# A layernorm, sparse-FFN, layernorm kernel: threshold steps moved to ScalarE and GpSimd within one stage, a shorter pipeline, and a reordered fill

## The reference, cut to what matters

```python
# x: (8, 512, 512) = 4096 tokens of 512
x = layernorm(x + x @ (W + delta_W).T)                       # LN1
z = x @ ternary_quant(W_syn).T + b_syn                       # 2048 wide
topv, _ = top_k(z, 204); thresh = topv[:, -1:]
hidden = where(z >= thresh, relu(z), 0.0)
out = hidden @ ternary_quant(W_out).T + b_out
x = layernorm(layernorm(x + out) * gamma + beta + x)         # LN2, residual, LN3 (no affine)
# ternary_quant(W): -1, 0 or +1 times mean(|W|), split at half that mean
```

## Time and profile before

| | us |
|---|---|
| median of 3 runs | 695.01 (693.21 to 698.05) |
| the profiled execution | 695.96 |
| span of its trace, first to last instruction | 694.2 |
| busy in the span: PE, DVE, ACT, POOL | 589.0, 537.7, 525.3, 349.2 |

### The profile page before, as it was taken

One profiled execution on the slowest core, in us unless ns is written; L12 is line 12 of the kernel. 1 busy time (PEld: TensorE's weight loads), 2 busy tenths in 40 slices (PEclk: granted clock), 3 DMA queues, 4 the chain that ended last, 5 costly groups with the idle time before them and its releaser, 6 DMA issues.

```text
span 694.2 us, 8155 instructions
## 1 busy us (share of the span) xinstructions
PE 589.0 (85%) x2374; PEld 256.9 (37%) x2374; DVE 537.7 (77%) x646; ACT 525.3 (76%) x659; POOL 349.2 (50%) x721
## 2 busy tenths in 40 slices
PE   0578896999999999999999999999999988055573
PEld 0233342444444444444444444444444433022221
DVE  4671856688888888888888888888888898677751
ACT  3436477679989988998888998998998988864322
POOL 0202731246556556556556556556556566565631
PEclk9877897999999999999999999999999999577786
DMA  9931121446464546464445554546444453233351
GB/s 343 389 100 47 22 55 36 85 77 112 101 122 91 123 69 143 70 134 87 110 89 121 91 122 91 123 91 122 92 91 93 91 92 76 45 77 76 78 104 46
DMA packets 184480, 71.61 MB, mean 103 GB/s; under 512 B 168048, under 2 KB 176240, under 8 KB 183792
## 3 DMA queue, kind: packets, MB, share of 16 engines
q1 hardware_dynamic: 184432, 71.07, 46.5%
HBM read 20.72 MB, written 8.39 MB: 42 GB/s over the span
## 4 chain that ended last, share of the span: by engine, by line
PE 28%; POOL 19%; issue 18%; DVE 6%; DMA 3%; ACT 1%; DVEq 0%; POOLq 0%; ACTq 0%
PE z_ps L805 8%; PE o_ps L821 8%; PE o_ps L815 8%; POOL nmean L328 4%; PE u_ps L791 4%; POOL rs L337 3%; DMA hT<-hh 3%; POOL x1b L345 2%; POOL b L340 2%; DVE m L650 2%; POOL x1g L349 1%; DVE w_sb L645 1%; DVE z_sb L703 1%; DVE hh L639 1%; ACT hh L504 1%
## 5 line engine op out<-in xcount | busy, mean ns | idle before, releaser
L480 ACT ACTIVATE junk<-z_sb,t_col 128x2048 f16<-128x2048 f32 x128 | 254.8, 1992 | 41.1 <-POOL t_col L383 41.1
L805 PE MATMUL z_ps<-t_syn,xhT 128*128 128x512 f16 x1024 | 226.2, 379 | 0.6 <-issue 0.6
L791 PE MATMUL u_ps<-weff,xT_sb 128*128 128x512 f32 x256 | 132.8, 667 | 32.8 <-DVE weff L578 16.8
L805 PEld LDWEIGHTS z_ps<-t_syn,xhT 128*128 128x128 f16 x1024 | 100.0, 98 | 131.8 <-issue 18.5
L345 POOL TENSOR_TENSOR x1b<-x1s,vecs 128x512 f32<-128x512 f32 x32 | 42.8, 1339 | 198.7 <-DVE z_sb L703 198.6
L815 PE MATMUL o_ps<-t_out,hT 128*128 128x512 f16 x512 | 123.6, 397 | 6.7 <-DMA hT<-hh 6.7
L821 PE MATMUL o_ps<-t_out,hT 128*128 128x512 f16 x512 | 117.4, 383 | 3.4 <-DMA hT<-hh 3.4
L669 DVE SCALAR_TENSOR_TENSOR z_sb<-z_ps,sc,bias_z 128x1024 f32<-128x1024 f32 x64 | 81.6, 1278 | 49.6 <-PE z_ps L805 49.6
L703 DVE SCALAR_TENSOR_TENSOR z_sb<-z_sb,thr 128x2048 f32<-128x2048 f32 x32 | 75.3, 2352 | 31.8 <-issue 16.3
L639 DVE TENSOR_TENSOR hh<-z_sb,hh 128x2048 f16<-128x2048 f32 x32 | 84.5, 2639 | 3.2 <-ACT hh L504 3.2
L791 PEld LDWEIGHTS u_ps<-weff,xT_sb 128*128 128x128 f32 x256 | 51.5, 212 | 89.6 <-issue 88.6
(11 more groups left out here) (114 smaller groups left out, 514.4 us busy)
## 6 DMA issues: line engine op xcount, KB each, us to landing
xT_sb<-in_xT SPq DMA_DIRECT2D x16, 512.0 KB, 4.8
out_y<-y_sb SPq DMA_DIRECT2D x32, 256.0 KB, 2.3
z_sb<-in_w_synT SPq DMA_DIRECT2D x4, 1024.0 KB, 13.0
z_sb<-in_w_outT SPq DMA_DIRECT2D x2, 1024.0 KB, 18.7
hh<-in_w_outT SPq DMA_DIRECT2D x2, 1024.0 KB, 13.7
weff<-in_wT SPq DMA_DIRECT2D x1, 1024.0 KB, 5.5
w_sb<-in_dwT SPq DMA_DIRECT2D x1, 1024.0 KB, 7.7
bias_z<-in_b_syn SPq DMA_DIRECT2D x1, 1024.0 KB, 17.4
```

Of the source, the lines that this page charges most:

```text
L480: a_.activation(junk[:, done[0] % 2, :], z_sb[:, t % ZS, :], ACT.Sign, bias=bias, scale=-1.0, accum_out=signs[:, t % CS:t % CS + 1]).then_ ...
L791: last = mm(u_ps[:, :], xT_sb[:, j, k, (t % 2) * P:(t % 2 + 1) * P], weff[:, k, :], start=k == 0, stop=k == KD - 1)
L805: last = mm(z_ps[:, c, b * BANK:(b + 1) * BANK], xhT[:, j, h * KD + k, :], t_syn[:, k, n0:n0 + BANK], start=k == 0 and h == 0, stop=k == K ...
```

## The change

- Lags. The threshold of a tile is found within one stage (only the fifth count falls in the next), so `L_SEL, L_MM3, L_LN2, L_OUT` go from 4, 5, 6, 7 to 2, 3, 4, 4 and the last stage from 38 to 35. `A_LN1` is 3.
- Threshold. The first two moves are made by ACT itself, one ACTIVATE on 128x1 each (`first_step`, `second_step`), with no damping and no gate. POOL makes the third and fourth (`update(t, 2)`, `update(t, 3)`) for the one tile, in 5 and 7 instructions, the gate in the last one only. `T_MIN` is gone and `SPREAD` is 1.295.
- Means. `mean_r` and `mean_v` take the place of `means`; POOL no longer waits for `hidden`.
- DVE order in a stage: `below`, `top8`, `lo_x`, `select`, `centre`, `general`, `hidden`, `add_v`, `evac` of the first half, `lo_h`, `evac` of the second, `add_r`.
- PE order: first half of `mm2`, `mm3_hi`, `flags`, `mm3_lo`, second half of `mm2`, `mm1`. The flag goes to the second half of `z_ps`.
- SP order: `transpose_x` of s+1, then both transposes of tile s-2, then the store.
- Fill, written out by hand. ACT makes Sign of W_syn plus the lower bound (`sign_syn`, 128x1024, fp16), DVE the part under it times -1, and an fp16 `tensor_tensor` max joins both. One of four |W_out| sums and the scaling of `vecs` move to DVE. The ternary of W_out is placed among the first tiles' work.

```diff
...
@@ -31,22 +31,21 @@
...
 ROUNDS = 5
-SPREAD = 1.2965
+SPREAD = 1.295
...
-L_SEL, L_MM3, L_LN2, L_OUT = 4, 5, 6, 7
-A_LN1, A_MM1 = 2, 3
-FIRST, LAST = -A_MM1, TILES - 1 + L_OUT
-ZS, XS, OS, CS = 6, 9, 3, ROUNDS
+L_SEL, L_MM3, L_LN2, L_OUT = 2, 3, 4, 4
+A_X, A_LN1, A_MM1 = 1, 3, 3
+LAST = TILES - 1 + L_OUT
+ZS, XS, OS = 6, 8, 3
...
-            for s in range(FIRST, LAST + 1):
-                if live(s - L_MM3):
-                    transpose_lo(s - L_MM3)
-                if s % 2 and 2 <= (s + 5) // 2 < PAIRS:
+            transpose_x(0)
+            load(2)
+            for s in range(LAST + 2):
+                if s % 2 and (s + 5) // 2 < PAIRS:
                     load((s + 5) // 2)
-                if live(s + A_LN1):
-                    transpose_x(s + A_LN1)
-                if live(s - L_OUT):
-                    store(s - L_OUT)
+                if live(s + A_X):
+                    transpose_x(s + A_X)
                 if live(s - L_SEL):
                     transpose_hi(s - L_SEL)
+                    transpose_lo(s - L_SEL)
+                if live(s - 1 - L_OUT):
+                    store(s - 1 - L_OUT)
             for j in range(2):
...
-            def means(s):
-                j, d, e = s % 2, s - L_LN2, s - L_OUT
-                wait(pool, r_made, upto(d))
-                wait(pool, v_made, upto(e))
-                wait(pool, sq_done[1], upto(d - 2))
-                wait(pool, sq_done[2], upto(e - 2))
-                g.tensor_scalar(nmean[:, j, :], sums[:, j, :], -1.0 / D, None, ALU.mult).then_inc(neg_means, 1)
+                g.tensor_scalar(start[:, 3:4], start[:, 2:3], SIGN_MID, start[:, 1:2], ALU.mult, ALU.add).then_inc(sigma_step, 1)
...
+            def mean_r(t):
+                pool.wait_ge(r_made, t + 1)
+                wait(pool, sq_done[1], t - 1)
+                g.tensor_scalar(nmean[:, 0, t % 2:t % 2 + 1], sums[:, 0, t % 2:t % 2 + 1], -1.0 / D, None, ALU.mult)\
...
+            def mean_v(t):
+                pool.wait_ge(v_made, t + 1)
+                wait(pool, sq_done[2], t - 1)
+                g.tensor_scalar(nmean[:, 1, t % 2:t % 2 + 1], sums[:, 1, t % 2:t % 2 + 1], -1.0 / D, None, ALU.mult)\
...
-                    g.tensor_tensor(b3[:, j:j + 1], nmean[:, j, 1:2], rs[:, j, 2:3], ALU.mult).then_inc(b3_ready, 1)
+                    pool.wait_ge(v_mean, e + 1)
+                    g.tensor_tensor(b3[:, j:j + 1], nmean[:, 1, e % 2:e % 2 + 1], rs[:, j, 2:3], ALU.mult).then_inc(b3_ready, 1)
...
+            def second_base(t):
...
+                pool.wait_ge(t_first, t + 1)
+                g.tensor_tensor(base[:, t % 2:t % 2 + 1], t_col[:, t % 2, 1:2], start[:, 4:5], ALU.add).then_inc(base_made, 1)
+            def update(t, r):
...
+                j = t % 2
+                signed, new, old = signs[:, j, r:r + 1], dev[:, j, r:r + 1], dev[:, j, r - 1:r]
+                before = slope[:, j, r - 1:r] if r > 2 else start[:, 2:3]
...
+                if r == 2:
+                    pool.wait_ge(counted, count_no(t, 1))
+                    made_old = step(g.tensor_scalar(old, signs[:, j, r - 1:r], SIGN_MID, None, ALU.add))
+                    pool.wait_ge(update_step, made_old)
+                pool.wait_ge(counted, count_no(t, r))
+                crossed = step(g.tensor_scalar(q[0], signed, SIGN_MID, old, ALU.add, ALU.mult))
+                made_dev = step(g.tensor_scalar(new, signed, SIGN_MID, None, ALU.add))
...
+                damp = step(g.tensor_scalar(q[1], q[0], 0.0, -DAMP, ALU.is_lt, ALU.mult))
+                move = new
+                if r == ROUNDS - 2:
+                    pool.wait_ge(update_step, made_dev)
+                    squared = step(g.tensor_scalar(q[2], new, new, None, ALU.mult))
...
+                damped = step(g.tensor_scalar(slope[:, j, r:r + 1], q[1], before, before, ALU.mult, ALU.add))
+                if r == ROUNDS - 2:
+                    pool.wait_ge(update_step, squared)
+                    move = q[3]
+                    far = step(g.tensor_scalar(move, q[2], GATE ** 2, new, ALU.is_gt, ALU.mult))
+                    pool.wait_ge(update_step, far)
+                    wait(pool, selected, t - 1)
+                else:
+                    pool.wait_ge(t_second, t + 1)
+                    pool.wait_ge(update_step, damped)
+                g.tensor_scalar(t_col[:, j, r + 1:r + 2], move, slope[:, j, r:r + 1], t_col[:, j, r:r + 1],
+                                ALU.mult, ALU.add).then_inc(updated[r - 2], 1)
+                pool.wait_ge(updated[r - 2], t + 1)
...
+            scales(-3)
+            bias_norm()
+            scales(-2)
+            sigma()
+            scales(-1)
+            for s in range(LAST + 1):
+                l, e = s - L_MM3, s - L_OUT
+                if live(l):
+                    mean_r(l)
+                if live(s):
+                    second_base(s)
+                if live(l + 1):
+                    if l + 1 == 0:
+                        pool.wait_ge(vecs_made, 1)
+                    add_bout(l + 1)
+                if live(s + A_LN1) or live(l) or live(e):
                     scales(s)
...
+                    add_beta(l)
+                if live(s):
+                    update(s, 2)
+                if live(l):
+                    mean_v(l)
+                if live(s):
+                    update(s, 3)
...
+            def sign_syn(i):
+                c, k = divmod(i, KD)
+                act.wait_ge(scaled, 1)
+                wait(act, t_syn_made, i - 3)
+                a_.activation(side[i % 4], syn_in[k][:, c * HALF:(c + 1) * HALF], ACT.Sign, bias=sc[:, 2:3])\
+                    .then_inc(over, 1)
...
+            def first_step(t):
+                act.wait_ge(counted, count_no(t, 0))
+                a_.activation(t_col[:, t % 2, 1:2], signs[:, t % 2, 0:1], ACT.Identity,
...
+                act.wait_ge(counted, count_no(t, 1))
+                act.wait_ge(base_made, t + 1)
+                a_.activation(t_col[:, t % 2, 2:3], signs[:, t % 2, 1:2], ACT.Identity,
+                              bias=base[:, t % 2:t % 2 + 1], scale=start[:, 2:3]).then_inc(t_second, 1)
...
+            sign_syn(6)
+            sum_nnz()
+            ln1_out(-2, 1)
+            hi_x(1)
+            sign_syn(7)
+            sum_out(0)
+            sum_out(1)
+            square1(-1, 2)
+            sum_out(2)
+            count(0, 0)
+            first_step(0)
+            ln1_out(-1, 2)
+            hi_x(2)
+            count(0, 1)
+            second_step(0)
+            square1(0, 3)
+            count(0, 2)
+            ln1_out(0, 3)
+            count(0, 3)
+            hi_x(3)
...
+            for s in range(1, LAST + 1):
+                l, e, a = s - L_MM3, s - L_OUT, s + A_LN1
+                if live(s):
+                    count(s, 0)
+                if live(s):
+                    first_step(s)
+                if live(a):
+                    square1(s, a)
+                if live(l):
+                    square2(s, l)
...
+                    count(s - 1, 4)
+                if live(s):
+                    count(s, 1)
+                    second_step(s)
+                    count(s, 2)
+                if live(a):
+                    ln1_out(s, a)
+                if live(s - 1):
+                    hi_h(s - 1)
+                if live(s):
+                    count(s, 3)
+                if live(a):
+                    hi_x(a)
+                if live(e):
+                    ln3_out(s, e)
+                if live(l):
+                    square3(s + 1, l)
...
+            def syn_weights(i):
+                c, k = divmod(i, KD)
+                below_lo = neg_syn[:, (i % 2) * HALF:(i % 2 + 1) * HALF]
+                wait(dve, t_syn_made, i - 1)
+                link(v.tensor_scalar(below_lo, syn_in[k][:, c * HALF:(c + 1) * HALF], sc[:, 2:3], -1.0, ALU.is_lt, ALU.mult))
+                dve.wait_ge(over, i + 1)
+                v.tensor_tensor(t_syn[:, k, c * HALF:(c + 1) * HALF], side[i % 4], below_lo, ALU.max).then_inc(t_syn_made, 1)
...
+            lo_x(1)
+            spread()
+            evac(0, 0)
+            evac(0, 1)
+            sum_out(3)
+            scale_vecs()
+            evac(1, 0)
+            out_part()
+            lo_x(2)
+            out_scale()
+            out_weights(0)
+            evac(1, 1)
+            out_weights(1)
+            evac(2, 0)
+            below(0)
+            top8(0)
+            select(0)
+            lo_x(3)
+            general(0)
+            hidden(0)
+            out_weights(2)
+            evac(2, 1)
+            lo_h(0)
+            out_weights(3)
+            for s in range(3, LAST + 1):
+                f, l, d, a = s - L_SEL, s - L_MM3, s - L_LN2, s + A_X
                 if live(f):
                     below(f)
                     top8(f)
+                if live(a):
+                    lo_x(a)
+                if live(f):
                     select(f)
...
+                if live(d):
```

(132 more changed lines are left out.)

243 lines of the change are left out of this document (75 added, 168 removed).

## The result

| | before | changed |
|---|---|---|
| median, us | 694.11 (689.02 to 698.05, 4 runs) | 658.62 (658.22 to 659.14, 4 runs) |
| span of the profiled execution | 694.2 | 656.4 |
| granted clock, mean over the span | 0.935 | 0.95 |

The ratio is 0.9493, 95% interval 0.9429 to 0.9557: 5.1% faster. The forecast was 650 us, a gain of 45; the measured time is 8.6 us longer and the gain 35.5 us. Sign and size hold, and the time lies in the range of 638 to 673, though just outside the 642 to 658 of the likeliest case alone.

What follows compares the result with a forecast made beforehand. PE was taken to bound the middle, so only the ends could move: fill 103.5, stages 4 to 28 440.5, stages 29 and 30 34, drain 70 give a 648 span; plus 1.8, 650 us, range 638 to 673.

Steps and rivals of the forecast that it cites:

- the likeliest case: The forecast itself without the rivals: 650 us, chance 0.64, 642 to 658 us if it alone holds.
- The fill ledger: Sum of DVE's work in the fill, up to the start of `mm2` of tile 4 at 103.5 us.
- T(4): T(s) is the start of `mm2` of tile s; for tile 4, the end of the fill, forecast at 103.5 us.
- DVE reaches its eighth max at 37.3, `spread` comes ahead of the evacs, first evac at 42.2: Early fill: ACT's Signs done at about 37.4, `spread` 1.7 us, first evac at 42.2 where before it was 44.54.
- from there DVE is full: Later fill, after `out_scale`: DVE's listed work and waits sum to 49.3 us, first `add_r` ending at about 104.
- the blocking row: Profile row where `means` on POOL took 2.29 us in place of 0.2: GpSimd stands still during DVE's `lo_h`.
- Rival 3: The fill gives nothing: first `mm3` waits for `t_out`, `mm2` of tile 4 13 us later, 663 us; chance 0.06.
- The four microseconds given to the fp16 max: In the fill, eight ternary pairs at 1.6 us instead of 2.11, max priced 0.75, save 4 us (or 0).
- the walk: One steady stage followed engine by engine: all fits under PE's 17.62 us, DVE with 0.9 left, longest loop 16.6.
- Rival 1: The stage stretches a little: with ACT steps of 0.6 each, about 18.3 us a stage, 667 us; chance 0.22.
- Rival 2: GpSimd's blocked time becomes the bound: 21.6 us a stage, 760 us, deciding from 19.2 a stage; chance 0.05.
- rival 4: The threshold search misses: one tile with a missed row runs 25 rounds, about 120 us, 770 us; chance 0.03.

## Why the prediction was right, and where it was off

**PE sets the middle, and the ends are where the time is: shown.** The stages are gapless, the window has PE at 300.00 of 300, and taking PE work away or adding work elsewhere moved the stage as a PE bound with a near second does. Part of the small error is luck: the fill and the drain came 14.0 us longer than forecast and the middle 5.6 shorter, and without the second the time would have been 664.

**The fill ledger failed.** T(4) came 10.7 late, and two of its terms were wrong. The step "DVE reaches its eighth max at 37.3, `spread` comes ahead of the evacs, first evac at 42.2" put nothing on the path but DVE and ACT. The first evac came at 44.05, 1.9 late (DVE had waited 1.96 for the last Sign of ACT), but the second at 50.84 instead of 43.5, because the list had no term for the first transpose, which was issued while W_out was still coming in. The run with late loads showed what it costs: the second evac 5.5 earlier, T(4) 5.1. The other is "from there DVE is full": update 2 of tile 0, priced 1.25 elsewhere and given no wait in this list, took 6.6 among W_out's ternary. I had used the blocking row for the steady stage and not for the fill, where DVE runs such instructions nearly without a pause. The rule that the forecast cited from the Trainium skill ("SBUF — State Buffer", "Terms": the loser fully blocks) covers this case as well; the trace agrees, with three steps of 1.42 to 2.21 us that end with DVE's instruction. A third omission stands behind both: the list had PE's work at the high clock, and the low level cost 2.7 us in the `mm3_lo` of tile 0 alone (6.29 for 3.63).

Rival 3, "the fill gives nothing", was nearer than its chance of 0.06: it had 663 and T(4) some 12 us late (its 13 is one too many by its own numbers), and by matmul work the fill gave 1.6 us and not 12. The four microseconds given to the fp16 max were at most one; the price of the instruction was a little high (0.61 for 0.75), and what waited behind it was left out.

**The stage fits under PE: right, by about a quarter of the margin,** 0.24 us where the walk had 0.9. The walk's order of events came out nearly as written: `below` waiting 0.29 for `update 3` in each stage, count 3 waiting for `hidden` and not for the threshold (ACT waited for `t_col` three times in all, each time in the fill), `mean_r` behind `below`. Timeline of the changed kernel:

```profile
303.52 0.37 POOL L387 TENSOR_SCALAR tmp<-signs,dev 128x1 f32<-128x1 f32 x1 [2.02 <-ACT junk L507]
...
305.60 0.34 POOL L406 TENSOR_SCALAR t_col<-tmp,slope,t_col 128x1 f32<-128x1 f32 x1
...
305.97 2.35 DVE L718 SCALAR_TENSOR_TENSOR w_sb<-z_sb,t_col 128x2048 f32<-128x2048 f32 x1 [0.29 <-POOL t_col L406]
306.02 2.38 POOL L332 TENSOR_SCALAR nmean<-sums 128x1 f32<-128x1 f32 x1
```

Mis-sized were `update 3`, 2.4 us (303.52 to 305.94) for 1.7, and `ok`, 0.94 for 0.22. The forecast counted five steps of `update 3` at 0.33, its longest chain; the trace has all seven one behind another, 0.21 to 0.37 each, their starts 0.22 to 0.46 apart. ACT's two small steps were 0.39 each, between the 0.2 that I took and the upper bound of 0.63. `lo_h`, 2.29 for 2.64, gave something back. Rival 1 (0.22) named the right place; its stage of 18.3 is 1.1 over the 17.24 at which the loop stands. Rival 2, 19.2 a stage and more, was far off; the run with three more steps shows only how a stage grows once the loop binds.

**The middle was 3.7 shorter than 25 x 17.62.** The 17.62 was a mean over 22 stages before. Twenty of them were 17.56 and two were 18.24 and 18.06, each with a wait of PE for `hT` (0.51 and 0.32). In the changed kernel PE waits for no `hT` in these stages; the new order of the transposes is the likely reason and was not tested. The step from 17.56 to 17.47 is in `mm1`. Before, it stood behind the flag, and from its start to that of `mm2` took 3.54 in 24 of 25 such places (3.70 in the earlier trace rows); once it stood behind `mm2`'s matmuls at the high clock, in the fill, and there took 3.43:

```profile
95.33 3.60 PE L791 MATMUL u_ps<-weff,xT_sb 128*128 128x512 f32 x8
98.77 7.07 PE L805 MATMUL z_ps<-t_syn,xhT 128*128 128x512 f16 x32
```

In the changed kernel it stands behind `mm2` in every stage and takes 3.43 there. So 0.1 us a stage is the place of `mm1` in PE's list.

**The drain** was right in mechanism (73.3 for 70). From T(31) `mm3_lo` of the last tile ended at 61.7 in place of 59.2; that the longer loop paced the stages before it is an argument from its length, and the run with `add_beta` behind the pick bears it out in part. From the last `add_r` to the end it was 11.6 and not 11.0; GpSimd now makes `x1g` behind the scales and `add_v` waits for it:

```profile
644.77 0.76 DVE L800 SCALAR_TENSOR_TENSOR o_ps<-o_ps,sc,x1b 128x512 f32<-128x512 f32 x1 [4.82 <-PE o_ps L902]
...
649.57 0.76 DVE L793 SCALAR_TENSOR_TENSOR o_ps<-o_ps,rs,x1g 128x512 f32<-128x512 f32 x1 [0.78 <-POOL x1g L361]
```

**The search** didn't miss: MAX8 ran 32 times, and rival 4 is out on these inputs.

## What to carry to other kernels

When the middle of a pipeline has its bound at 100%, count the stages of lag: each that goes shortens the drain, and the price is the slack in the middle. Here the drain lost 33 us, with two stages less before the last tile's `mm3` and three less before its output. Measure that slack by adding work to each engine in turn; two opposite experiments (more in the loop, less on the bound) gave the same 0.24 us, where a sum of durations gave 0.9. And price the fill with what else is in flight there, transfers and instructions that hold up GpSimd, not with the durations of the steady state; and look at the clock there, since a wait of PE can cost a second time in the matmuls behind it (6.29 us for 3.63).
